# One gather or scatter of a kind on the way: waits in GpSimd's queue of indirect DMAs

## What is computed

```
x = x + attn(layernorm(x))
h = layernorm(x)
p = softmax(h @ gate_w.T)                  # 8 experts
v, i = top_k(p, 2)
out = 0
for e in range(8):
    y = silu(h @ w1[e] + b1[e]) @ w2[e] + b2[e]      # 128 -> 512 -> 128
    out = out + y * (v where i == e, else 0)
x = x + out
```

## Time and profile before

| what | us |
|---|---|
| timed runs | 557.63, 551.62, 554.52 |
| median of the timed runs | 554.52 |
| profiled execution, first to last instruction (its span) | 604.2 |
| profiled execution, a time of its own beside the span | none given |
| POOL busy in the span | 361.1 |
| PE busy in the span | 513.4 |
| DVE busy in the span | 441.4 |
| ACT busy in the span | 302.2 |

### The profile page before, as it was taken

The page is one execution under the profiler, slowest core; times in us unless marked ns, Lnnn a source line. Parts: engine busy times, 40 slices in busy tenths (PEclk is TensorE's granted clock), DMA queues, the critical chain, the costliest instruction groups (busy, mean ns, idle before and its releaser), DMA issues. The chain is left out here.

```text
span 604.2 us, 10225 instructions
## 1 busy us (share of the span) xinstructions
PE 513.4 (85%) x2821; PEld 408.8 (68%) x2821; DVE 441.4 (73%) x1396; ACT 302.2 (50%) x671; POOL 361.1 (60%) x322
## 2 busy tenths in 40 slices
PE   2999899999999999967794699889999988992982
PEld 2778777777777778756673478767777866871761
DVE  6788888878888886764773488668788876881774
ACT  2445333333333333234882577567667755761752
POOL 3332467777777776876017102888788788855361
PEclk9999899999999997967898799999999998996896
DMA  8627968858888511164266487879889988993653
GB/s 281 198 71 232 356 242 295 292 179 293 293 292 299 211 39 33 39 237 145 88 232 239 158 292 248 253 241 277 256 268 298 301 265 250 308 319 94 224 165 119
DMA packets 65609, 134.77 MB, mean 223 GB/s; under 512 B 8208, under 2 KB 24976, under 8 KB 60560
## 3 DMA queue, kind: packets, MB, share of 16 engines
q1 hardware_dynamic: 51984, 116.79, 54.6%
q0 software_dynamic: 13568, 17.32, 12.4%
HBM read 29.83 MB, written 63.09 MB: 154 GB/s over the span
## 5 line engine op out<-in xcount | busy, mean ns | idle before, releaser
L894 POOL DMA_INDIRECT rows_in<-yrow,slots x128 | 125.4, 980 | 63.3 <-issue 34.8
L1444 DVE TENSOR_TENSOR hl<-hf,hh 128x512 fp32r<-128x512 f32 x156 | 108.6, 697 | 18.9 <-ACT hh L857 13.9
L1442 DVE CAST hh<-hf 128x512 fp32r<-128x512 f32 x144 | 64.0, 445 | 52.9 <-ACT hf L853 41.9
L853 ACT ACTIVATE hf<-qp,wst 128x512 f32<-128x512 f32 x104 | 72.4, 696 | 54.5 <-PE qp L495 29.8
L952 POOL DMA_INDIRECT xres<-rows_out,slots x48 | 78.3, 1632 | 14.6 <-issue 14.6
L943 POOL DMA_INDIRECT yrow<-rows_out,slots x40 | 40.5, 1013 | 55.9 <-DMA rows_out<-yo 38.9
L753 ACT ACTIVATE yrow<-xres,nb,rs 128x128 f32<-128x128 f32 x64 | 26.3, 482 | 63.6 <-DVE nb L1123 63.6
L853 ACT ACTIVATE hf<-kvp,wst 128x512 f32<-128x512 f32 x52 | 36.1, 695 | 41.1 <-PE kvp L495 18.2
L493 PE MATMUL qp<-xT_h,wst 128*128 128x512 f32 x104 | 46.2, 445 | 2.4 <-DVE xT_l L1402 1.8
L488 PE MATMUL gate_wo<-first_sb,yTs 128*128 128x128 f32 x156 | 25.7, 291 | 26.1 <-ACT yTs L865 24.3
L902 POOL TENSOR_TENSOR rs<-ve,half 128x8 f32<-128x8 f32 x20 | 33.8, 1690 | 23.4 <-DVE ve L1006 22.6
(11 more groups left out here) (224 smaller groups left out, 1440.6 us busy)
## 6 DMA issues: line engine op xcount, KB each, us to landing
wst<-wres SPq DMA_DIRECT2D x39, 1030.5 KB
rows_out<-tail SPq DMA_DIRECT2D x28, 1280.0 KB
xg<-rows_in SPq DMA_DIRECT2D x39, 272.0 KB
rows_out<-yo SPq DMA_DIRECT2D x39, 256.0 KB
wraw<-in_w_experts SPq DMA_DIRECT2D x8, 512.0 KB, 4.3
out_x<-xres SPq DMA_DIRECT2D x16, 256.0 KB
rows_in<-tail SPq DMA_DIRECT2D x11, 272.0 KB, 4.0
rows_in<-yrow,slots POOLq DMA_INDIRECT x128
```

The costliest lines, as they stand in the source:

```text
L853: nc.scalar.activation(hf[n % N_H][:], hbank(t, c), ACT.Silu, bias=b_part(wst[t % NBUF], c, 1)).then_inc(s["h_silu"], 1)
L894: nc.gpsimd.indirect_dma_start(rows_in, bass.IndirectOffsetOnAxis(ap=slots[:, f, k, j:j + 1], axis=0), rows_of(f)[:, j, :], None).then_inc ...
L1442: nc.vector.tensor_copy(hh[n % N_H][:], hf[n % N_H][:]).then_inc(s["h_high"], 1)
L1444: nc.vector.tensor_tensor(hl[n % N_H][:], hf[n % N_H][:], hh[n % N_H][:].bitcast(F32), ALU.subtract).then_inc(s["h_low"], 1)
```

## The change

Three things change, all in GpSimd's queue. The scatters of batch 13 wait, from the second on, for the one before to land. Those of batches 14 and 15 alternate, and each waits for the one before of its own batch. In `gather(b)` the four plain gathers of the second choice and the four of the first choice alternate, and each but the first of a kind waits for the one before of its kind in that batch. The first pair of a batch waits for nothing of the batch before.

```
-            for f in range(NB - 3, NB):
-                to_experts(f, 0)
-                to_experts(f, 1)
+            def one_scattered(f, n):
+
+                if n > 0:
+                    after(pool, f"scat{f % N_YROW}", (f // N_YROW * SUB * TOP_K + n) * 16, alone=True)
+                to_experts(f, n // SUB, range(n % SUB, n % SUB + 1))
+
+            for n in range(SUB * TOP_K):
+                one_scattered(PAIR - 1, n)
+            for n in range(SUB * TOP_K):
+                for f in range(PAIR, NB):
+                    one_scattered(f, n)
...
                 for j in range(SUB):
+                    after(pool, f"got1_{b % N_GOT}", (b // N_GOT * SUB + j) * 16 if j else 0, alone=True)
                     nc.gpsimd.indirect_dma_start(
                         got[b % N_GOT][:, j, :], None, rows_out,
                         bass.IndirectOffsetOnAxis(ap=slots[:, b, 1, j:j + 1], axis=0)).then_inc(s[f"got1_{b % N_GOT}"], 16)
-                for j in range(SUB):
+                    after(pool, f"got0_{b % N_GOT}", (b // N_GOT * SUB + j) * 16 if j else 0, alone=True)
                     if plain(b):
                         nc.gpsimd.indirect_dma_start(
                             first_got[b - NB + LAST_PLAIN][:, j, :], None, rows_out,
```

## The result

The changed kernel takes 656.18 us in the median of its timed runs (652.38 to 663.6), the kernel before 553.07 beside it: a ratio of 1.1822, with a 95% interval from 1.1769 to 1.1876. One run of the four, 663.6, was disturbed: it is in the median and not in the ratio. Slower was forecast, at 614 us; the time lies 42 above that and 6 above the end of the range. The profiled execution of the change spans 654.6 us.

The account below looks back on a forecast made before the run. GpSimd's queue and the expert stage were taken to run at almost equal paces; additive waits 54, plain 5, batch 13's scatters 0, those of 14 and 15 5, slack -5: 59 us on 554.5, say 614 us, range 575 to 650.

Parts of the forecast that it names:

- What bounds it: GpSimd (13.1 us a batch) and the expert stage (12.9) run at almost equal paces, so GpSimd has little slack.
- Landing of an additive gather: Batches 0 to 11: landing taken as 3.9 us, so 36 waits stretch cycles from 3.14 to 4.65 us, 54 us.
- low end: Additive gather landing after 3.2 us, with nothing beside it at the end; the 36 waits then cost 29 us.
- high end: Additive gather landing after 5.05 us, a weights load's time from issue to use; the 36 waits then cost 96 us.
- Rival 4: Additive landings beside weights loads stay near 5 us: 671 us at the worst, 640 halfway; chance 17%.
- rival 1: Additive gathers land within 2.4 us, so their waits cost nothing: 560 us, 1% slower, or no change; chance 8%.
- Restart: On GpSimd's queue, the next issue starts 0.75 us after what it waited for has ended.
- The plain gather fits in between; its own wait never ends last: Additive batches 0 to 11: plain gathers' waits add nothing beside those of the additive gathers.
- The first pair of a batch: Batches 0 to 11: it has no wait, leaving three waits a batch; a pair takes 3.14 us to issue.
- Plain batches: Batches 12 to 15: cycles grow from 2.54 to 2.95 us, twelve waits x 0.41 = 5 us.
- Scatters: Batch 13's 13 us are hidden by GpSimd's idle time, so 0; batches 14 and 15 count 5 us.
- Slack and tail, -5: GpSimd's slack in the timed run, between 0 and 7.6 us, taken as 5, also covering the final adds.

Follow-up runs that it names:

- in series: The changed kernel with all its waits, but a batch's four plain gathers go before its four first-choice ones, one gather on the way: 810.76 us.
- plain batches first: The changed kernel, but the four batches whose first choice is gathered plainly are 0 to 3 instead of 12 to 15: 653.70 us.
- weights loads light: The changed kernel, but from tile 3 on the load of the weights brings the biases alone: 627.24 us.
- weights, row loads, stores light: The changed kernel, but from tile 3 on weights loads bring only biases, and a tile's row load and store move a quarter of the rows: 608.67 us.
- in series, weights loads light: The changed kernel with four plain gathers, then four first-choice ones, one on the way, and weights loads cut to the biases from tile 3: 777.61 us.

## Why the prediction was right in its mechanism and wrong in its size

*What bounds it.* Right: GpSimd's queue and the expert stage run at two paces that are almost equal, and once GpSimd is slower VectorE's adds hand its lateness to PE, from batch 5 on ("from about batch 6 on", it said). The judgement that the stalls of the earlier trace rows were the recording's was right too.

*Landing of an additive gather: the step that failed.* It said "I take 3.9", because "when GpSimd lags, the expert stage stops and loads become rarer". The cycle was to be 4.65 us and was 5.35: 36 x 0.70 = 25 of the 42 us. The landings that were waited for take 4.48 us in the mean instead of 3.9, that is 0.58 of the 0.70; the other 0.12 come from 9 of the 36 gathers, which started later than the usual 0.76 us after that landing. Its low end was right: with no expert traffic the cycle is 4.12 (3.2 + 0.75 gives 3.95). Its high end was not a bound: 14 of the 48 landings take more than 5.05 us, up to 6.62, and the weights loads themselves 4.6 to 7.1.

The reason given for moving only a little above the low end was wrong. In batches 0 to 4 the expert stage does not stop at all, and 3 or 4 weights loads fall into each batch instead of 2. Only from batch 5 on do loads become rarer, one or two a batch, since VectorE now waits at its adds. Over the twelve batches the tiles to be loaded and stored stay as many as they were (26 weights loads, 24 before), however long they take. A straight line through the lengths of the twelve batches against their weights loads gives 16.4 us and 1.64 for each load in the change, and 25.6 and 1.80 in series, where the first three batches have five loads each and the others one or two; these are estimates from twelve scattered points each. The runs show the same as what a batch takes beyond its quiet length. The quiet length is 16.1 us in alternating order (plain batches first). In series I put it together from quiet cycles: 3 x 3.25 plain (median of the plain batches there) + 1.3 + 3 x 4.0 additive + 2.4 = 25.5.

| kernel | batch, us | beyond quiet |
|---|---|---|
| the change | 19.9 | 3.8 |
| weights loads light | 18.1 | 2.0 |
| weights, row loads, stores light | 16.7 | 0.6 |
| in series | 29.5 | 4.0 |
| in series, weights loads light | 27.7 | 2.2 |

Half as long again, the batch in series pays the same 4 us for its 2.2 tiles in the mean, and the light weights loads take 1.8 and 1.9 from the two. So the additive batches' 79.5 us are 12 x (16.1 - 13.3) = 34 for quiet landings and 12 x 3.8 = 46 for meeting the traffic of the tiles. Rival 4, "landing beside the weights loads stays near 5", was nearest: 640 for halfway, 671 at the worst.

The Trainium skill, "DMA: Bandwidth & Descriptors", section "Anatomy of one DMA — SWDGE (gpsimd) path", gave the estimated 2.15 us of rival 1. The quickest additive landing measured is 3.1 us, the quickest plain one 2.4, so both lie above it and rival 1 falls by measurement.

*Restart.* Right: 0.72 us in the chain, 0.75 used.

*"The plain gather fits in between; its own wait never ends last".* Wrong as a sentence, right in the sum. The waits of the changed kernel name the plain landing as the last releaser of plain gathers 19 times (13 into `yrow`, 6 into `more_got`), but leaving out the plain waits saves nothing (647.92 and 644.91 us).

*The first pair of a batch.* The prediction gave it 3.14 us; it takes 3.87, since the register loads lie bare behind the last wait. This would have cost 12 x 0.73 = 9 us, and is balanced, by luck, by a batch of before that takes 13.3 us and not the 12.55 of the one batch that the step was read from. Moving the loads gave 10 to 13 us back over all batches.

*Plain batches.* Predicted 5, measured 13.4. A cycle is 3.34 us and not 2.95, since the landing is 2.5 and not the 2.2 read from the end of the traffic; that is 12 x 0.39 = 4.7 more, and most of the rest (3.1) lies at the three changes of batch, 2.38 us from last to first issue instead of 1.35.

*Scatters.* Batch 13 at 0: right. Batches 14 and 15: 8.6 us for 5, since the landings met the expert stage (the waits stretch the sixteen issues by 12.3 us and not by 4) and the cover was not there.

*Slack and tail, -5.* Wrong: there was next to none, -0.6. The wait of 12.74 us before batch 14 in the earlier trace rows was the recording's, as the prediction said; so were the 4.26 and 3.33, from which it took its 5. The 648 that it gave for the profiled execution lies near the 654.6 by luck: it was counted with the stalls, and there were none.

Together: 25 in the additive cycles, 8.4 in the plain batches (13.4 for 5), 3.4 before the first gather (8.4 for 5) and 4.4 in slack and tail make 41 of the 42 us. Where only plain gathers wait, their late landings could be the expert traffic's doing or that of the additive gathers ahead of them. The last four batches of the kernel with plain batches first speak for the traffic: without it a plain gather with an additive one on the way lands within 2.94 us. No run took the traffic away where only plain gathers wait, so for that kernel it is not shown.

## What to carry to other kernels

A wait for the DMA before turns a queue of transfers into a row of landings. Price it at the quiet landing plus the restart, and add what the other traffic costs for each unit of its own work (here 1.6 to 1.8 us for a tile, an estimate): a slower queue does not make these units fewer, and as long as nothing hands the lateness on, the other stage does not slow down at all. If the number of transfers on the way must be bounded, two instead of one gave back 82 of 92 us here (647.92 to 565.97). What an engine does between its last wait and its next issue is no longer hidden once the wait ends late, so put it ahead of the wait.

## What the runs showed of the hardware

Behind the expert stage's loads an additive gather of 128 rows lands 3.2 to 3.7 us after its issue (median 3.26; 3.1 is the quickest of all runs), a plain one after 2.4 to 2.9 (median 2.52); that a plain one is on the way beside it costs the additive one next to nothing (a cycle of 4.12 us in the quiet batches, against a median of 4.08 and 3.93 at the least in series). Under the loads and stores of the expert stage both reach 6 us and more. One recorded execution was 50 us longer than another of the same kernel, with two stalls that the other did not have; why is not shown.
